# Shared rows scattered into the table of sums, and first-choice blocks scattered onto them with addition

## The chip, the cores and the metric

The kernel runs on one core of a Trainium2 chip, in one launch. Its time is the device time of that core in microseconds (us); smaller is better. The engines are named as in the profile: PE is TensorE (PEld its weight loads), DVE is VectorE, ACT is ScalarE, POOL is GpSimd and SP is SyncE, which here only issues DMAs.

## The reference, cut to what matters

Input x has 8 x 2048 = 16384 tokens of D = 256 float32 values. A time-mixing layer (an RWKV recurrence with four 256 x 256 products) gives a residual, and a mixture-of-experts layer follows. Only the second matters for the change:

```python
probs = softmax(xf @ router_w)            # 8 experts
topw, topi = top_k(probs, 2)              # a first and a second choice per token
h  = silu(einsum('nd,edf->nef', xf, w1))
ye = einsum('nef,efd->ned', h, w2)
routed = einsum('ne,ned->nd', combine, ye)      # weight1 * ye[first] + weight2 * ye[second]
shared = sigmoid(xf @ gate_w) * ((silu(gate) * up) @ shared_down)
x = x + layernorm(routed + shared)
```

So each token ends as a sum of three rows of 256 values: the shared row, the first choice's weighted row and the second choice's weighted row. The norm and the residual come after the sum.

## The kernel before

**First stage (about 0 to 1083 us).** The tokens go through in NCH = 32 chunks of 512. For each chunk the time-mixing layer, the router and the shared expert are computed; every float32 product is made of three matmuls with split operands. For each choice the kernel works out a position for every token in a table that is sorted by expert (`place`, L1151). POOL then scatters rows with indirect DMAs of 128 rows each. `scatter` (L541) writes the normalised token row, with its weights, its second-choice position, its token number and two statistics (272 floats), to `d_xd[0]` at the first-choice position and to `d_xd[1]` at the second-choice position. `shared_scatter` (L553) writes the shared row (256 floats) to `d_xs` at the first-choice position. The gaps between the experts' regions are filled with padding rows by SP (`pads`, L393), whose position fields are out of bounds, so that they are skipped in later scatters.

**Second stage (about 1083 us to the end).** The tables are read in blocks of 256 rows: NB1 = 71 blocks of first choices and then 71 of second choices. `tabx` holds each block's first row and `tabp` its expert. Per block w: SP loads 256 rows of `d_xd` into one of 12 buffers `xb` (`load_block`, L425); PE transposes them (`block_in`), ACT and DVE split them into a high and a low part and copy the expert's weights; PE multiplies (`block_hidden`), ACT applies silu, PE multiplies again (`block_out`) into one of three PSUM buffers `outB`; DVE's `y_out` (L1399) multiplies by the weight and adds a row that SP has loaded into one of 12 buffers `yb` (`load_result`, L435).

For a first-choice block, that loaded row is the shared row from `d_xs`; POOL's `sums_out` (L588) scatters the sum, in two indirect DMAs of 128 rows, into the table of sums `d_ys` at the second-choice positions. For a second-choice block, the loaded row is from `d_ys`; ACT takes squares, POOL computes the scale (`last_scale`), DVE finishes (`final`), and POOL scatters to the output (`tokens_out`).

The order within every engine is the program order. A wait on a semaphore holds back all that stands behind it on that engine. PE may start `block_out(w)` only when `y_out(w - 3)` is done, because there are three `outB`. SP may load into `xb` or `yb` buffer w only when the scatter of block w - 12 has landed (`landed`, L362). The first `load_result` of the second choices (w = NB1 = 71) waits until the scatters of the last 12 first-choice blocks have landed, since the rows that it reads may come from any of them.

Of the kernel before, what the change touches and what calls it, by code (L numbers as in the profile page):

```python
# [5 lines left out]
ALU = mybir.AluOpType  # L6
ACT = mybir.ActivationFunctionType
AX_X = mybir.AxisListType.X
F32 = mybir.dt.float32
# [5 lines left out]
P = 128  # L15
TC = 512
NT = TC // P
# [3 lines left out]
BLK = 256  # L21
XW = 272


def rwkv_moe(nc, x, decay, u_in, mix_k, mix_v, mix_r, wkT, wvT, wrT, woT, router, w1, w2,
# [9 lines left out]
    B, T, D = x.shape  # L35
    E = w1.shape[0]
    H = D // P
    N = B * T
    NCH = N // TC
    assert D == 256 and E == 8 and T == CARRY * TC  # L40
    RW = E + 2
    CAP = N + BLK
# [4 lines left out]
    NB1 = NF + E - 1  # L47
    NB = 2 * NB1
    NBP = NB1 + 1
    NX = NYB = 12  # L50
    LY = 2
    LT = 6
# [4 lines left out]
    x_v = x.rearrange("b (c j p) d -> (b c) p j d", j=NT, p=P)  # L57
    out_r = out.rearrange("b t d -> (b t) d")
    d_xd = [nc.dram_tensor(f"d_xd{s}", [E * CAP + BLK, XW], F32).ap() for s in range(2)]
    d_xs = nc.dram_tensor("d_xs", [E * CAP + BLK, D], F32).ap()  # L60

    d_ys = nc.dram_tensor("d_ys", [E * CAP + BLK, D], F32).ap()

    with ExitStack() as ctx:
# [80 lines left out]
        ixs = sb("ixs", [P, 2, 2 * NT], U32)  # L145
# [85 lines left out]
        s_T1 = sem("s_T1")  # L231
# [32 lines left out]
        s_h2 = sem("s_h2")  # L264
# [18 lines left out]
        s_scy = sem("s_scy")  # L283
# [5 lines left out]
        s_pad = sem("s_pad")  # L289
        s_xb = [sem(f"s_xb{i}") for i in range(NX)]  # L290
        s_yo = [sem(f"s_yo{i}") for i in range(NYB)]
        s_yl = [sem(f"s_yl{i}") for i in range(NYB)]
# [10 lines left out]
        s_y = sem("s_y")  # L303
# [21 lines left out]
        def n(c, per, k):  # L325
            return c * per + k

        def rows(t):
# [5 lines left out]
        xb = [old[i // 5][:, i % 5 * 2 * XW:(i % 5 + 1) * 2 * XW] for i in range(10)] + [t[:, 0:2 * XW] for t in old[2:4]]  # L334
        xb = [t.rearrange("p (j d) -> p j d", j=2) for t in xb]
        sil = [flat(t)[:, i * 2 * D:(i + 1) * 2 * D] for t, i in ((al, 0), (be, 0), (al, 1))]
        hidB, outB = PS[2:5], PS[5:8]
        yb = [flat(t)[:, i * 2 * D:(i + 1) * 2 * D].rearrange("p (j d) -> p j d", j=2)
              for i in range(2) for t in (kk, vv, tr, dl, nx, x1)]
# [22 lines left out]
        def landed(w):  # L362

            return s_yo[w % NYB], 32 * (w // NYB + 1)
# [6 lines left out]
        @block.sync  # L371
        def _(sp):
            def load_weights(m):
                for i, src in enumerate(loads[m]):
                    w = src.shape[2]
                    dst = flat(stage[m])[:, i * H * w:(i + 1) * H * w]
                    sp.dma_start(dst.rearrange("p (a n) -> p a n", a=H), src).then_inc(s_wld[m], 16)

            sp.dma_start(xin[:, :, :], x_v[0]).then_inc(s_x, 16)
            with nc.allow_non_contiguous_dma(reason="small vectors, once"):  # L380
                for i, v in enumerate((mix_k, mix_v, mix_r)):
                    sp.dma_start(vec[:, i, :], v.rearrange("o t (a p) -> p (o t a)", p=P)).then_inc(s_vec, 16)
                load_weights(0)
                for i, v in enumerate((u_in, decay)):
                    sp.dma_start(vec[:, 3 + i, :], v.rearrange("(a p) -> p a", p=P)).then_inc(s_wu, 16)
                load_weights(1)
                sp.wait_ge(s_const, NCONST)
                sp.dma_start(rwf[:, :, 0:E], src_mat(router)).then_inc(s_rwf, 16)
                sp.dma_start(rwf[:, :, E:E + 1], src_mat(gate_w)).then_inc(s_rwf, 16)
                load_weights(2)  # L390
                load_weights(3)

            def pads(e):  # L393

                sp.wait_ge(s_zt, 2)
                for rows, width in ((d_xd[0], XW), (d_xd[1], XW), (d_xs, D), (d_ys, D)):
                    pad = rows[e * CAP:e * CAP + BLK, :].rearrange("(p j) d -> p j d", p=P)
                    sp.dma_start(pad, zt[:, 0:width].unsqueeze(1).to_broadcast([P, 2, width])).then_inc(s_pad, 16)

            sp.wait_ge(s_nx, n(0, NT, NT))  # L400
            sp.dma_start(xin[:, :, :], x_v[1]).then_inc(s_x, 16)
            sp.wait_ge(s_wl, NP)
            sp.dma_start(x1[:, :, :], x_v[0]).then_inc(s_xr, 16)
            for i in range(NCH + 4):
                if i % 2 == 0 and i // 2 < E:

                    raw = wel[:, i // 2 * 1024:(i // 2 + 1) * 1024].bitcast(F32)
                    if i:
                        sp.wait_ge(s_we, 32 * (i // 2))
                    for k, src in enumerate((w1[i // 2], w2[i // 2])):  # L410
                        sp.dma_start(raw[:, k * H * D:(k + 1) * H * D].rearrange("p (a n) -> p a n", a=H), src_mat(src)
                                     ).then_inc(s_we, 16)
                if 1 < i < NCH:
                    sp.wait_ge(s_nx, n(i - 1, NT, NT))
                    sp.dma_start(xin[:, :, :], x_v[i]).then_inc(s_x, 16)
                if 0 < i - 3 < NCH:
                    sp.wait_ge(s_h2, n(i - 3 - 1, NT, NT))
                    sp.dma_start(x1[:, :, :], x_v[i - 3]).then_inc(s_xr, 16)
                if 0 <= i - FIRST_PAD <= E:
                    pads(i - FIRST_PAD)  # L420
            sp.wait_ge(s_pad, 16 * 4 * (E + 1))
            sp.wait_ge(s_tab, 2)
            sp.wait_ge(s_sct[0], 16 * NT * NCH)

            first_row = {}  # L425

            def load_block(b):
                if b >= NX:
                    sp.wait_ge(*landed(b - NX))
                s = b // NB1  # L430
                r = sp.value_load(tabx[0:1, s, b % NB1:b % NB1 + 1], min_val=0, max_val=E * CAP)
                first_row[b % (LT + 1)] = r
                sp.dma_start(xb[b % NX], d_xd[s][bass.ds(r, BLK), :].rearrange("(p j) d -> p j d", p=P)
                             ).then_inc(s_xb[b % NX], 16)

            def load_result(w):

                if w >= NYB:
                    sp.wait_ge(*landed(w - NYB))
                rows_in = d_xs if w < NB1 else d_ys  # L440
                sp.dma_start(yb[w % NYB], rows_in[bass.ds(first_row[w % (LT + 1)], BLK), :].rearrange("(p j) d -> p j d", p=P)
                             ).then_inc(s_yl[w % NYB], 16)

            for b in range(NB + LY):
                if b == NB1:
                    sp.wait_ge(s_tab, 4)
                    sp.wait_ge(s_sct[1], 16 * NT * NCH)
                if b == 10:
                    sp.wait_ge(s_up, n(NCH - 1, 2, 2))
                if b < NB:  # L450
                    load_block(b)
                due = [b - LY] if LY <= b < NB + LY and (b - LY) % NB1 >= LT - LY else []
                if b % NB1 == LT and b < NB:
                    due = list(range(b - LT, b - LY + 1))
                for w in due:
                    if w == 0:
                        sp.wait_ge(s_scy, 16 * NT * NCH)
                    if w == NB1:
                        for k in range(NB1 - NYB, NB1):
                            sp.wait_ge(*landed(k))  # L460
                    load_result(w)

            for w in range(NB - NYB, NB):
                sp.wait_ge(*landed(w))

        @block.gpsimd
        def _(pool):
            g = nc.gpsimd
# [85 lines left out]
            def shared_scatter(m):  # L554
                pool.wait_ge(s_pl, n(m, NPL, L_IX))
                for j in range(NT):
                    pool.wait_ge(s_ys, n(m, NT, j + 1))
                    g.indirect_dma_start(d_xs, bass.IndirectOffsetOnAxis(ap=ixs[:, m % 2, j:j + 1], axis=0),  # L558
                                         ysh_of(m)[:, j, :], None).then_inc(s_scy, 16)

            scale_in(0)
# [25 lines left out]

            def sums_out(w):  # L588

                pool.wait_ge(s_y, 2 * (w + 1))  # L590
                for j in range(2):
                    g.indirect_dma_start(d_ys, rows_at(w, j, C_POS), yb[w % NYB][:, j, :], None,  # L592
                                         bounds_check=E * CAP - 1, oob_is_err=False).then_inc(s_yo[w % NYB], 16)

            def last_scale(q):

# [362 lines left out]
        def _(dve):  # L959
            V = nc.vector  # L960
# [360 lines left out]
            w, y, z = NCH - 3, NCH - 2, NCH - 1  # L1321
# [76 lines left out]

            def y_out(w):  # L1399
                dve.wait_ge(s_yp, w + 1)  # L1400
                dve.wait_ge(s_yl[w % NYB], 16 * (w // NYB + 1))
                col = C_W + w // NB1
                for j in range(2):
                    t = yb[w % NYB][:, j, :]
                    V.scalar_tensor_tensor(out=t, in0=outB[w % 3][:, j * D:(j + 1) * D], scalar=xb[w % NX][:, j, col:col + 1],  # L1405
                                           in1=t, op0=ALU.mult, op1=ALU.add).then_inc(s_y, 1)
# [345 lines left out]
```

## Time and profile before

| what | value |
|---|---|
| median of three runs | 1598.68 us (1597.98 to 1603.28) |
| the profiled execution | 1603.3 us, of which the span is 1601.5 us |
| mean granted PE clock | 0.976 of 2.4 GHz |
| PE busy | 1513.8 us (95%) |
| DVE busy | 1377.2 us (86%) |
| ACT busy | 1336.3 us (83%) |
| POOL busy | 1079.9 us (67%) |
| DMA, software queue (issued by POOL) | 32064 packets, 86.04 MB, 14.6% of 16 engines |
| DMA, hardware queue (issued by SP) | 92368 packets, 126.13 MB, 26.1% of 16 engines |

The span is the time from the first to the last instruction of the profiled execution; the time of the execution is 1.8 us longer. Shares over the whole span mix three stretches with different limits: the chunks (to about 1083 us), the first choices (1083 to 1337 us) and the second choices (from 1337 us), so the text reads the stretches one by one. Busy time of POOL for an indirect DMA is the time in which it writes the DMA's descriptors, not the time in which the data move.

### The profile page before, as it was taken

The page shows a single profiled execution, that of the slowest core. Times are in us where ns is not written, and L with a number is a line of the kernel's source. Part 1 is how long each engine was busy: PE and PEld are TensorE (multiplying, and loading weights), DVE is VectorE, ACT ScalarE, POOL GpSimd, SP SyncE. Part 2 cuts the span into 40 slices and gives each one's busy share as a digit, 9 for nine tenths or more (in the row PEclk, how much of TensorE's full clock was granted, in tenths as well). Part 3 has the DMA queues.
Part 4 walks back from the last instruction along what each step waited for, and adds up shares of the span by engine and source line. Part 5 has one row for each costly group of instructions (what it writes and reads, how often), then busy time and mean ns, then how long its engine had stood idle before and what let it go on. Part 6 is the DMA issues. An engine that isn't in the chain of part 4 may idle for free.

```text
span 1601.5 us, 35130 instructions
## 1 busy us (share of the span) xinstructions
PE 1513.8 (95%) x9960; PEld 1360.9 (85%) x9960; DVE 1377.2 (86%) x3140; ACT 1336.3 (83%) x2768; POOL 1079.9 (67%) x1168
## 2 busy tenths in 40 slices
PE   5899999999999999999999999689999998999992
PEld 4778888888888888888888888578999998999992
DVE  5899998999999999999999888856877777999993
ACT  5688998899889988999898888756777777999993
POOL 1256677767776766677677766766666664888886
PEclk9999999999999999999999999889999999999996
DMA  4114333533322222222222222138777764777771
GB/s 125 41 55 132 118 113 115 171 106 126 108 95 82 83 85 91 79 86 87 88 82 82 91 72 73 65 100 283 238 238 244 247 207 136 229 223 229 235 239 55
DMA packets 124619, 214.41 MB, mean 134 GB/s; under 512 B 19975, under 2 KB 67338, under 8 KB 124432
## 3 DMA queue, kind: packets, MB, share of 16 engines
q1 hardware_dynamic: 92368, 126.13, 26.1%
q0 software_dynamic: 32064, 86.04, 14.6%
q8 instruction: 86, 1.41, 0.4%
q14 instruction: 101, 0.83, 0.2%
HBM read 116.37 MB, written 99.39 MB: 135 GB/s over the span
## 4 chain that ended last, share of the span: by engine, by line
PE 62%; DVE 12%; issue 10%; POOL 9%; ACT 1%; DMA 1%; DVEq 1%; POOLq 0%; SPq 0%; ACTq 0%
PE PS L1474 53%; POOL d_ys L592 8%; PE PS L1466 3%; PE PS L1538 2%; PE PS L1536 2%; PE PS L1692 2%; DVE rkl L1446 1%; DVE shl L1446 1%; PE PS L1708 1%; DVE x L1405 1%; DVE ysh L1413 1%; DVE dl L1405 1%; DVE xin L1413 1%; POOL out L610 1%; DVE tr L1405 1%
## 5 line engine op out<-in xcount | busy, mean ns | idle before, releaser
L551 POOL DMA_INDIRECT d_xd<-h2n,ixs x248 | 310.3, 1251 | 193.2 <-DVE h2n L1193 127.0
L1474 PE MATMUL PS<-hTh,wqh 128*128 128x512 f32 x768 | 305.1, 397 | 12.3 <-DVE hTl L1114 10.3
L1474 PE MATMUL PS<-hTl,wqh 128*128 128x512 f32 x768 | 305.0, 397 | 0.0
L1474 PE MATMUL PS<-hTh,wql 128*128 128x512 f32 x768 | 305.0, 397 | 0.0
L1474 PEld LDWEIGHTS PS<-hTh,wqh 128*128 128x128 f32 x768 | 145.9, 190 | 46.4 <-issue 10.9
L1474 PEld LDWEIGHTS PS<-hTh,wql 128*128 128x128 f32 x768 | 145.4, 189 | 34.2
L1474 PEld LDWEIGHTS PS<-hTl,wqh 128*128 128x128 f32 x768 | 145.7, 190 | 33.2
L558 POOL DMA_INDIRECT d_xs<-ysh,ixs x124 | 130.6, 1054 | 45.8 <-issue 45.8
L1708 PE MATMUL PS<-weh,h2h 128*128 x380 | 106.4, 280 | 0.0
L1708 PE MATMUL PS<-weh,h2l 128*128 x380 | 106.3, 280 | 0.0
L1708 PE MATMUL PS<-wel,h2h 128*128 x380 | 106.1, 279 | 0.0
L1474 PE MATMUL PS<-h2h,wgh 128*128 128x512 f32 x248 | 103.4, 417 | 0.0
L1452 DVE TENSOR_TENSOR h2l<-al,h2h 128x512 fp32r<-128x512 f32 x95 | 65.6, 691 | 43.6 <-ACT h2h L953 43.6
L1474 PE MATMUL PS<-h2l,wgh 128*128 128x512 f32 x248 | 97.8, 394 | 0.0
L1474 PE MATMUL PS<-h2h,wgl 128*128 128x512 f32 x248 | 97.5, 393 | 0.0
L1692 PE MATMUL PS<-rkh 128*128 128x256 f32 x284 | 86.3, 304 | 5.7 <-DVE rkl L1446 5.5
L1474 PE MATMUL PS<-woh,rkh 128*128 128x256 f32 x256 | 76.4, 298 | 15.0 <-DVE rkl L1211 15.0
L1692 PE MATMUL PS<-hTh,shh 128*128 128x256 f32 x284 | 86.3, 304 | 3.5 <-DVE shl L1446 3.5
L1692 PE MATMUL PS<-rkh,rkl 128*128 128x256 f32 x284 | 80.8, 284 | 0.0
L1692 PE MATMUL PS<-rkl,rkh 128*128 128x256 f32 x284 | 80.7, 284 | 0.0
L1692 PE MATMUL PS<-hTl,shh 128*128 128x256 f32 x284 | 80.6, 284 | 0.0
L1041 DVE TENSOR_TENSOR_SCAN ee<-negw,ee,kk 128x512 f32<-128x512 f32 x64 | 78.7, 1272 | 1.9 <-ACT kk L647 0.6
(330 smaller groups left out, 5665.8 us busy)
## 6 DMA issues: line engine op xcount, KB each, us to landing
xin<-in_L_attn_x SPq DMA_DIRECT2D x32, 512.0 KB, 4.3
x<-in_L_attn_x SPq DMA_DIRECT2D x32, 512.0 KB
wqh<-d_xd SPq DMA_DIRECT2D x60, 272.0 KB, 3.5
wql<-d_xd SPq DMA_DIRECT2D x60, 272.0 KB, 2.9
d_xd<-zt SPq DMA_DIRECT2D x18, 272.0 KB
wel<-in_L_ffn_w SPq DMA_DIRECT2D x16, 256.0 KB, 5.1
d_xd<-h2n,ixs POOLq DMA_INDIRECT x248, 2.6
kk<-d_xs SPq DMA_DIRECT2D x12, 256.0 KB
```

What stands on the lines that cost most here:

```text
L551: g.indirect_dma_start(d_xd[s], bass.IndirectOffsetOnAxis(ap=ixs[:, m % 2, k:k + 1], axis=0), h2n_of(m)[:, j, :], None).then_inc(s_sct[s], 16)
L558: g.indirect_dma_start(d_xs, bass.IndirectOffsetOnAxis(ap=ixs[:, m % 2, j:j + 1], axis=0), ysh_of(m)[:, j, :], None).then_inc(s_scy, 16)
L592: g.indirect_dma_start(d_ys, rows_at(w, j, C_POS), yb[w % NYB][:, j, :], None, bounds_check=E * CAP - 1, oob_is_err=False).then_inc(s_yo[w ...
L1041: V.tensor_tensor_scan(ee[:, a, 1:TC + 1], negw[:, a:a + 1].to_broadcast([P, TC]), kk[:, a, :], ee[:, a, 0:1], ALU.add, ALU.max).then_inc( ...
L1405: V.scalar_tensor_tensor(out=t, in0=outB[w % 3][:, j * D:(j + 1) * D], scalar=xb[w % NX][:, j, col:col + 1], in1=t, op0=ALU.mult, op1=ALU. ...
L1413: V.tensor_scalar(xk[v % 4][:, 0, :], xb[w % NX][:, 0, 0:D], xb[w % NX][:, 0, C_EXT:C_EXT + 1], xb[w % NX][:, 0, C_EXT + 1:C_EXT + 2], ALU ...
L1446: V.tensor_copy(w1l[t % 2], wel[:, bass.ds(base, H * D)]).then_inc(s_w1l, 1)
L1452: V.tensor_tensor(aTl[u % 3], sil[u % 3], aTh[u % 3].bitcast(F32), ALU.subtract).then_inc(s_al2, 1)
L1466: ins = nc.tensor.transpose(bank[a][:, j * P:(j + 1) * P], src[:, j, a * P:(a + 1) * P], ident[:, :])
L1474: ins = mm_(out_ap, l, r, start=(k == 0), stop=(k == len(todo) - 1))
L1692: ins = mm_(hidB[u % 3][:, f * D:(f + 1) * D], l, r, start=(k == 0), stop=(k == len(todo) - 1))
L1708: ins = mm_(outB[w % 3][:, j * D:(j + 1) * D], l, r, start=(k == 0), stop=(k == len(todo) - 1))
```

## The change

The table `d_xs` goes. In the first stage, `shared_scatter` writes the shared rows into `d_ys`, at the second-choice positions (columns NT to 2 NT of `ixs`, where it used columns 0 to NT). First-choice blocks no longer load anything into `yb`: `y_out` writes weight x product there by a `tensor_scalar`, and `sums_out` scatters it with `compute_op=ALU.add`, so that the DMA adds the row to what `d_ys` holds. The wait for all the shared scatters moves from SP (ahead of the first `load_result`) to POOL (ahead of the first `sums_out`). The wait that buffer `yb` is free again moves, for first-choice blocks, from SP to DVE. Second-choice blocks are as before, and SP's list of result loads starts with w = 71.

```diff
-    d_xs = nc.dram_tensor("d_xs", [E * CAP + BLK, D], F32).ap()
...
-                for rows, width in ((d_xd[0], XW), (d_xd[1], XW), (d_xs, D), (d_ys, D)):
+                for rows, width in ((d_xd[0], XW), (d_xd[1], XW), (d_ys, D)):
...
-            sp.wait_ge(s_pad, 16 * 4 * (E + 1))
+            sp.wait_ge(s_pad, 16 * 3 * (E + 1))
...
-                rows_in = d_xs if w < NB1 else d_ys
-                sp.dma_start(yb[w % NYB], rows_in[bass.ds(first_row[w % (LT + 1)], BLK), :].rearrange("(p j) d -> p j d", p=P)
+                sp.dma_start(yb[w % NYB], d_ys[bass.ds(first_row[w % (LT + 1)], BLK), :].rearrange("(p j) d -> p j d", p=P)
                              ).then_inc(s_yl[w % NYB], 16)
...
-                due = [b - LY] if LY <= b < NB + LY and (b - LY) % NB1 >= LT - LY else []
-                if b % NB1 == LT and b < NB:
+                due = [b - LY] if b - LY >= NB1 + LT - LY else []
+                if b == NB1 + LT:
                     due = list(range(b - LT, b - LY + 1))
                 for w in due:
-                    if w == 0:
-                        sp.wait_ge(s_scy, 16 * NT * NCH)
...
             def shared_scatter(m):
-                    g.indirect_dma_start(d_xs, bass.IndirectOffsetOnAxis(ap=ixs[:, m % 2, j:j + 1], axis=0),
+                    g.indirect_dma_start(d_ys, bass.IndirectOffsetOnAxis(ap=ixs[:, m % 2, NT + j:NT + j + 1], axis=0),
                                          ysh_of(m)[:, j, :], None).then_inc(s_scy, 16)
...
             def sums_out(w):
+                if w == 0:
+                    pool.wait_ge(s_scy, 16 * NT * NCH)
                 pool.wait_ge(s_y, 2 * (w + 1))
                 for j in range(2):
                     g.indirect_dma_start(d_ys, rows_at(w, j, C_POS), yb[w % NYB][:, j, :], None,
-                                         bounds_check=E * CAP - 1, oob_is_err=False).then_inc(s_yo[w % NYB], 16)
+                                         bounds_check=E * CAP - 1, oob_is_err=False, compute_op=ALU.add).then_inc(s_yo[w % NYB], 16)
...
             def y_out(w):
                 dve.wait_ge(s_yp, w + 1)
-                dve.wait_ge(s_yl[w % NYB], 16 * (w // NYB + 1))
                 col = C_W + w // NB1
+                if w < NB1:
+                    if w == 0:
+                        dve.wait_ge(s_h2, n(NCH - 1, NT, NT))
+                        dve.wait_ge(s_T1, n(NCH - 1, 2, 2))
+                    if w >= NYB:
+                        dve.wait_ge(*landed(w - NYB))
+                    for j in range(2):
+                        V.tensor_scalar(yb[w % NYB][:, j, :], outB[w % 3][:, j * D:(j + 1) * D], xb[w % NX][:, j, col:col + 1],
+                                        None, ALU.mult).then_inc(s_y, 1)
+                    return
+                dve.wait_ge(s_yl[w % NYB], 16 * ((w - NB1) // NYB + 1))
```

## Rows read from the trace of the kernel before

**Rows 1.** Windows by stage: us, busy time (instructions) per engine, granted clock, DMA share, GB/s.
```profile
1080.00:1120.00 40.00, 36.16 (x285) 35.53 (x285) 25.08 (x50) 27.00 (x48) 26.19 (x26) 0.93 0.84 283
1200.00:1320.00 120.00, 120.00 (x1032) 120.00 (x1031) 88.59 (x184) 88.47 (x148) 81.28 (x74) 1.00 0.74 236
1320.00:1360.00 40.00, 35.65 (x283) 34.97 (x282) 29.28 (x66) 31.23 (x75) 17.12 (x19) 0.91 0.40 130
```

**Rows 2.** Waits, 1200 to 1320 us: who waited for whom, total us, times, longest.
```profile
POOL d_ys L592 <- issue: 33.3, 68, 0.7
DVE h2l L1452 <- ACT h2h L953: 20.4, 24, 1.0
ACT hTh L941 <- PE PS L1673: 11.1, 19, 0.6
```

**Rows 3.** Timeline, POOL, in step with the blocks: start, us, instruction [idle before <- releaser].
```profile
1318.27 0.98 POOL L592 DMA_INDIRECT d_ys<-vv,wql  x1 [0.72 <-issue]
1319.56 1.23 POOL L592 DMA_INDIRECT d_ys<-vv,wql  x1 [0.30 <-issue]
1321.52 0.99 POOL L592 DMA_INDIRECT d_ys<-tr,wql  x1 [0.72 <-issue]
```

**Rows 4.** Timeline, POOL, late and without a wait between blocks.
```profile
1285.11 0.99 POOL L592 DMA_INDIRECT d_ys<-tr,wql  x1 [1.81 <-DVE dl L1405]
1286.40 0.99 POOL L592 DMA_INDIRECT d_ys<-dl,wql  x1 [0.30 <-issue]
1287.69 0.99 POOL L592 DMA_INDIRECT d_ys<-dl,wql  x1 [0.30 <-issue]
1288.99 0.99 POOL L592 DMA_INDIRECT d_ys<-nx,wgh  x1 [0.30 <-issue]
```

**Rows 5.** Tile d_xs: duration ns min/median/max, first and last start.
```profile
L558 POOL DMA_INDIRECT d_xs<-ysh,ixs x124: 956/963/1877, 152.5 to 1082.8; - x124
L398 SPq DMA_DIRECT2D d_xs<-zt x9: 643/658/1723, 151.6 to 406.1; - x9
DMA to landing us min/median/max: 3.1/3.8/4.9
```

**Rows 6.** Windows at the end of the first choices, and where only loads run.
```profile
1318.00:1332.00 14.00, 14.00 (x123) 14.00 (x122) 8.42 (x18) 10.63 (x18) 8.95 (x8) 1.00 0.13 41
1335.00:1341.00 6.00, 3.83 (x18) 3.86 (x19) 4.71 (x11) 3.25 (x9) 0.00 (x0) 0.50 0.98 333
```

**Rows 7.** Timeline, from the last scatter of first choices to the second choices.
```profile
1329.34 1.28 POOL L592 DMA_INDIRECT d_ys<-nx,wgh  x1 [0.30 <-issue]
1332.02 0.33 SPq L441 DMA_DIRECT2D x<-d_ys  x1
1334.94 0.88 DVE L1405 SCALAR_TENSOR_TENSOR x<-PS,wgl,x 128x256 f32<-128x256 f32 x2 [5.19 <-DMA x<-d_ys]
1335.73 0.40 DVE L1413 TENSOR_SCALAR ysh<-wgl 128x256 f32<-128x256 f32 x1
1337.17 0.55 PE L1692 MATMUL PS<-rkh 128*128 128x256 f32 x1 [4.35 <-DVE rkl L1446]
1341.79 0.32 PE L1708 MATMUL PS<-weh,shh 128*128 x1
```

**Rows 8.** Timeline, start of the first choices.
```profile
1088.01 0.96 POOL L558 DMA_INDIRECT d_xs<-xin,ixs  x1 [0.30 <-issue]
1090.55 0.33 SPq L441 DMA_DIRECT2D kk<-d_xs  x1
1092.32 0.35 PE L1692 MATMUL PS<-hTh,shh 128*128 128x256 f32 x1 [0.76 <-DVE shl L1446]
1095.91 0.87 DVE L1405 SCALAR_TENSOR_TENSOR kk<-PS,wqh,kk 128x256 f32<-128x256 f32 x2
1097.60 1.00 POOL L592 DMA_INDIRECT d_ys<-kk,wqh  x1 [3.07 <-DVE kk L1405]
1115.77 0.36 PE L1692 MATMUL PS<-rkh 128*128 128x256 f32 x1 [0.35 <-DVE rkl L1446]
1129.82 0.36 PE L1692 MATMUL PS<-rkh 128*128 128x256 f32 x1 [0.45 <-DVE rkl L1446]
```

## The prediction

> **What bounds the kernel now.** The change lies in the first choices, 1083 to 1337 us, and touches the first stage only in where rows go; so I read the busy time by window first, then the waits of that stretch, then POOL's timeline, and last the two seams, where the stretch begins and where it ends.
>
> Between 1200 and 1320 us PE is busy for 120.00 of 120 us at the full clock [rows 1]. POOL issues 74 indirect DMAs there, two per block, so 37 blocks take 120 us: 3.24 us per block. The waits agree that nothing holds PE: none has PE as the waiter, DVE's largest is 20.4 us for ACT, ACT's is for PE [rows 2]. This stretch is bound by PE alone.
>
> POOL needs care. Its timeline looks full: pairs of DMAs, 0.72 us between blocks and 0.30 us inside a pair [rows 3]. The reader may take that for a bound, since the wait view calls all of it "issue" [rows 2]. But when POOL was 1.81 us late it went from one block to the next with 0.30 us, and each DMA took 0.99 us [rows 4]. So a pair costs 2 x (0.99 + 0.30) = 2.58 us when POOL does not wait, against the block's 3.24 us. POOL has 0.66 us to spare per block, 0.33 us per DMA. It follows DVE in step, and its second DMA is stretched to 1.23 us, which costs nothing.
>
> The DMA engines are 74% busy at 236 GB/s [rows 1]. Where only loads run they reach 333 GB/s at 0.98 [rows 6]. They are a resource with a quarter to spare.
>
> **Part by part, first stage.** The shared scatter keeps its count of 128 DMAs of 128 rows; its row has a median of 963 ns and only the index column changes [rows 5]. The nine padding stores of `d_xs` go, 0.66 us of SP's queue each, between 152 and 406 us [rows 5]; SP has no arithmetic and nothing waits on that stretch of its queue but the next x load, which is a chunk ahead. Both: 0.
>
> **Loads removed.** 71 loads of 256 KB go from SP, at 0.33 us of issue each and a landing of 3.1 to 4.9 us [rows 5, 8]. They are issued blocks ahead: in the whole stretch from 1200 to 1320 us no wait names them [rows 2]. At the start, SP's first `d_xs` load went at 1090.55 us, and DVE used it at 1095.91 us, right after PE's product [rows 8]. Nothing is gained there but DMA time. Per block: 256 KB at 333 GB/s is 262,144 / 333,000 = 0.79 us.
>
> **DVE.** Two `scalar_tensor_tensor` of 0.44 us (0.88 us for two) become two `tensor_scalar`; the nearest row, the same width from SBUF, has 0.40 us [rows 7]. I take a gain of 0.08 us per block, bounds 0 and 0.2. DVE has 88.59 of 120 us of work [rows 1], so it is hidden: 0.
>
> **Moved waits.** POOL's new wait for all shared scatters: the last one was issued at 1088.01 us, and SP's load of 1090.55 us stood behind that same semaphore; POOL's first sum goes at 1097.60 us [rows 8]. It passes with 7 us to spare; had the cover gone, the pairs of all 71 blocks would queue behind it. DVE's new wait for the landing of block w - 12: behind it stand the splits of the next block, for which PE waits. It has 12 x 3.24 = 39 us of cover against a landing of a few us. Both 0, as long as POOL and the DMA engines keep pace.
>
> **The addition: POOL.** The trace has no scatter with addition. Lower end: it costs what the same scatter without addition costs, 0.99 us [rows 4]. Upper end: it costs two such DMAs, because each row names two things to read, 1.98 us. A saving is excluded, since it still names every row. PE's pace is lost from 3.24 / 2 - 0.30 = 1.32 us on. I take 1.15 us, nearest to its own row with addition for the second address, and so no cost in the steady stretch; the second of a pair takes 1.23 us today and nobody waits [rows 3].
>
> **The addition: DMA engines.** A block now moves 272 KB of x, 256 KB of shared rows and 256 KB of sums. The busy time is 0.74 x 3.24 = 2.40 us per block [rows 1]; the two loads are 541 KB at 333 GB/s, 1.62 us, so the plain scatter has 0.78 us. Afterwards: x at 0.84 us plus a scatter with addition at k x 0.78 us. Read and write of the same rows is k = 2, which gives 2.40 us again, the same load as today. k = 1 gives 1.62 us. PE's pace is lost from k = (3.24 - 0.84) / 0.78 = 3.1 on; the trace has no row that bounds k from above. I take 2.
>
> **The seam to the second choices.** This is the one place where the scatter is on the path. The last scatter is issued until 1330.62 us, the load of block 71 goes at 1332.02 us, DVE gets it at 1334.94 us, and PE stands still for 4.35 us and then runs at half clock (1.2 GHz) until 1341.79 us [rows 7]. Here the longer POOL span counts twice (two DMAs of the last pair): 2 x (1.15 - 0.99) = 0.3 us. The landing could grow too, but 41 GB/s from 1318 to 1332 us [rows 6] say that the last blocks are nearly all padding and move next to nothing; I add 0.3 us, bounds 0 and 2. Sum: 0 + 0.3 + 0.3 - 0.1 (DVE's shorter step) = +0.5 us.
>
> **Sum.** The profiled execution took 1603.3 us (span 1601.5), 4.6 us above the median of 1598.7; it is the slowest of the three runs. On it: 1603.3 + 0.5 = 1603.8. Carried to the median: 1598.7 + 0.5 = 1599.2, rounded to 1599.5 us. The case's own range is 1595 to 1604.
>
> **Rivals.**
>
> *POOL becomes the bound (slower).* Mechanism: writing descriptors for a row that is read twice takes long enough that a pair exceeds 3.24 us; POOL then sets the pace of all 71 first-choice blocks, the lag piles up in the 12 buffers, and the first load of the second choices has to wait it out, so all of it is paid. It decides from 1.32 us per DMA. At one and a half times today's span, 1.48 us, a pair takes 2 x 1.78 = 3.56 us: 71 x 0.32 = 23 us, 1622 us. At 1.98 us it is 4.56 us: 71 x 1.32 = 94 us, 1693 us. For it: the slack is only a third of a span. Against it: the span hardly varies with the rows (963 ns for the shared rows, 990 ns with a bounds check [rows 4, 5]), which speaks for a large fixed part.
>
> The Trainium skill speaks for this rival: "GPSIMD Engine Reference", section "When to use GPSIMD", has one core write the read descriptors and another the write descriptors, and "Collectives: The Full Stack", section "The bandwidth ceiling", has an add on the DMA path take two read descriptors where a copy takes one. By these the reading side's share would double, and the time would fall anywhere between this rival's ends; no run here shows a DMA with addition yet.
>
> *The DMA engines become the bound (slower).* If read, add and write of a row cost k = 4 plain rows, a block needs 0.84 + 3.12 = 3.96 us: 0.72 us over, and over the some 67 blocks that move data (the last four by the 41 GB/s do not) 48 us, 1647 us. For it: rows of 1 KB are short, and an addition must wait for its own read. Against: at k = 2 a quarter of the engines' time stays free.
>
> *Faster.* What the removed loads crowd would come earlier: PE's gaps at the start, 0.76 + 0.35 + 0.45 us [rows 8], and at the seam 4.35 us and the half clock from 1337.17 to 1341.79 us (2.3 us lost). All gone, that is 8.2 us: 1590.5 us. Against: the gaps at the start are waits for DVE's and ACT's splits, and the seam's wait is for a scatter that stays.
>
> **How the numbers follow.** No change (POOL keeps pace): 0.45. POOL bound: 0.35. DMA bound: 0.14. Faster: 0.06. The likeliest single case gives the time, 1599.5 us, though the two slower ones together weigh a little more. A measurement here tells 0.3%, 4.8 us, from no change. Of the first case 0.42 falls within that, 0.02 above, 0.01 below; of POOL bound 0.03 within (a pair barely above the pace); of the faster case 0.05 beyond and 0.01 within. That is faster 0.06, same 0.46, slower 0.48. The range must take in most of POOL's case and the nearer part of the DMA engines': 1594 to 1665 us leaves out about 0.04 below and 0.14 above.
>
> **What would show it.** POOL's indirect DMA on `d_ys` in the first choices: a span under 1.32 us and idle time of 0.4 us or more between pairs bears me out; 0.30 us everywhere with a longer span is the POOL rival. A block period of 3.24 us between 1200 and 1320 us with PE at 120 of 120 is the core of the forecast. A DMA share near 0.74 shows k = 2; near 1.0 with DVE waiting for landed scatters shows the DMA rival. At the seam, PE's gap should be 4 to 6 us. I am wrong if PE shows gaps inside the first choices.

## The result and the profile after

The changed kernel takes 1637.76 us (median of 4 runs, 1633.45 to 1640.75) against 1598.86 us for the kernel before in the same comparison: ratio 1.0218, 95% interval 1.0191 to 1.0245. It is 2.2% slower, and the interval is far from no change. The profiled executions took 1639.4 us (span 1637.6) and 1603.3 us (span 1601.5), 36.1 us apart; the text below works on these two.

The windows by stage of the changed kernel (us, busy time and instructions of PE, PEld, DVE, ACT, POOL, granted clock, DMA share, GB/s):

```profile
1160.00:1200.00 40.00, 40.00 (x345) 40.00 (x344) 30.12 (x62) 29.29 (x50) 33.60 (x22) 1.00 0.83 141
1200.00:1320.00 120.00, 109.91 (x914) 106.70 (x914) 83.39 (x164) 78.74 (x132) 100.49 (x65) 1.00 0.85 142
1320.00:1360.00 40.00, 28.30 (x234) 27.07 (x232) 18.66 (x36) 19.96 (x33) 33.60 (x22) 0.93 0.75 124
```

The stretch from the first scatter of sums to the stop of PE at the seam, in the changed kernel and then in the kernel before:

```profile
1098.25:1351.95 253.70, 238.63 (x2000) 233.36 (x1998) 181.86 (x364) 172.25 (x286) 213.00 (x134) 1.00 0.83 138
```
```profile
1097.60:1332.82 235.22, 234.26 (x2002) 233.19 (x2000) 175.28 (x364) 172.03 (x286) 157.65 (x142) 1.00 0.72 231
```

PE, full in the middle of the first choices before [rows 1], now has gaps: none from 1160 to 1200 us, 10 of 120 us after that. The window from 1320 us also holds the first 8 us of the wait at the seam. Over the whole stretch PE is idle for 15.1 us, and was for 1.0 us. POOL issued 74 DMAs in 120 us before; now it issues 65, and is busy for 100 us. The reader should see the order: POOL is at its limit from the start, PE only later, because the 12 buffers let POOL fall behind for a while.

POOL's timeline in the same stretch, and its last pair with the load behind it:

```profile
1256.06 1.55 POOL L590 DMA_INDIRECT d_ys<-x,wql  x1 [0.30 <-issue]
1257.92 1.55 POOL L590 DMA_INDIRECT d_ys<-kk,wql  x1 [0.30 <-issue]
1259.78 1.55 POOL L590 DMA_INDIRECT d_ys<-kk,wql  x1 [0.30 <-issue]
...
1365.11 1.55 POOL L590 DMA_INDIRECT d_ys<-nx,wgh  x1 [0.30 <-issue]
1368.12 0.33 SPq L439 DMA_DIRECT2D x<-d_ys  x1
1370.89 0.88 DVE L1413 SCALAR_TENSOR_TENSOR x<-PS,wgl,x 128x256 f32<-128x256 f32 x2 [22.39 <-DMA x<-d_ys]
1373.12 0.55 PE L1700 MATMUL PS<-rkh 128*128 128x256 f32 x1 [21.17 <-DVE rkl L1454]
```

Each DMA with addition takes 1.55 us where the plain one took 0.99 us [rows 4], and there are 0.30 us between any two, also between blocks, where POOL used to stand idle for 0.72 us [rows 3]. The first scatter of the first choices starts at 1098.25 us, the last ends at 1366.66 us: 268.4 us for 71 blocks, 3.78 us each. Before, it was 1097.60 to 1330.62 us [rows 7, 8]: 233.0 us, 3.28 us each. The difference, 35.4 us, is the loss. The start came 0.65 us later. The seam itself is the same: 1.4 us from the last scatter's end to the load, 2.8 us to DVE (2.9 before), 2.2 us to PE, as before [rows 7]; only PE's gap is longer (21.17 us, not 4.35), since it now waits out the lag that POOL had built up. So 16.8 us of the loss are a longer wait at the seam and 14.1 us are PE's gaps before it; PE's busy time in the stretch grew by the other 4.4. From PE's restart to the end of the span there are 264.5 us, and were 264.3 us.

Some of the waits (who waited for whom, us in total, times, longest), POOL's of 1085 to 1390 us, PE's and SP's of the stretch up to the seam, show how the lag reaches PE:

```profile
POOL d_ys L590 <- issue: 37.8, 124, 0.3
```
```profile
PE PS L1681 <- DMA wql<-d_xd: 5.2, 7, 1.5
SPq L430 <- DMA d_ys<-x,wql: 18.9, 6, 3.9
```

After its first scatter POOL waits for nothing that is longer than its own 0.30 us. PE's transposes (L1681) wait for x rows, 13.6 us in all (this line and three like it). SP in turn waits at its own queue for scatters to `d_ys` (L430): each x load stands behind the landing of the scatter 12 blocks earlier, which POOL has not got to.

### The profile page after: what moved, and what is told of

It is laid out like the page before. It is cut to its first block, busy times and chain, and to the rows that moved or that the text cites. A ratio compares the mean times of both kernels' runs of the same rounds, so it can differ in the third digit from the quotient of the medians.

```text
span 1637.6 us, 34898 instructions
## 1 busy us (share of the span) xinstructions
PE 1521.6 (93%) x9960; PEld 1364.0 (83%) x9960; DVE 1383.4 (84%) x3140; ACT 1336.3 (82%) x2768; POOL 1143.9 (70%) x1168
## 3 DMA queue, kind: packets, MB, share of 16 engines
q0 software_dynamic: 45696, 86.05, 20.2%
q8 instruction: 86, 1.41, 0.4%
## 4 chain that ended last, share of the span: by engine, by line
PE 66%; DVE 12%; issue 9%; POOL 5%; DMA 4%; ACT 2%; DVEq 1%; SPq 0%; POOLq 0%; ACTq 0%
PE PS L1482 52%; PE PS L1700 4%; POOL d_ys L590 3%; PE PS L1474 3%; PE PS L1716 2%; PE PS L1546 2%; PE PS L1544 2%; PE PS L1681 1%; DVE rkl L1454 1%; DVE shl L1454 1%; DVE ysh L1421 1%; DVE xin L1421 1%; POOL out L608 1%; DVE tr L1413 1%; DVE x L1413 1%
## 5 line engine op out<-in xcount | busy, mean ns | idle before, releaser
L554 POOL DMA_INDIRECT d_ys<-ysh,ixs x124 | 130.7, 1054 | 45.8 <-issue 45.5
```

Of the source, the lines that this page charges most:

```text
L554: g.indirect_dma_start(d_ys, bass.IndirectOffsetOnAxis(ap=ixs[:, m % 2, NT + j:NT + j + 1], axis=0), ysh_of(m)[:, j, :], None).then_inc(s_ ...
```

## Experiments

The theory after the result: POOL's time to write the descriptors of an addition is the pace of the first choices. Its rival: the DMA engines that read, add and write the rows are the limit (their share rose from 0.74 to 0.85). A second rival: the moved waits cost something of their own.

A measure that all the runs below share is the length of the first choices, from POOL's first scatter of sums to PE's first matmul after the seam: 239.6 us before, 274.9 us changed. In the comparisons below the kernel before had medians of 1602.9 to 1603.6 us, 4 to 5 us above the one that the expectations start from, so the ratios say more than the absolute times.

**e1, the addition left out.**

```diff
-   oob_is_err=False, compute_op=ALU.add)
+   oob_is_err=False)
```

> The changed kernel with a plain scatter instead of one with addition (the shared rows are lost from the sums). POOL theory (writing descriptors for an addition takes 1.55 us per DMA, 3.70 us per pair, against PE's 3.24 us per block): the span falls back to 0.99 us and the time to about 1599 us (1596 to 1603). Rival, the rest of the change costs something (the moved waits on DVE and POOL): more than 1604 us. The DMA theory says 1599 us too.

Measured: 1603.14 us, ratio 1.0005 (0.9979 to 1.0030).

```profile
1200.00:1320.00 120.00, 120.00 (x1032) 120.00 (x1030) 89.01 (x185) 89.13 (x148) 81.36 (x74) 1.00 0.53 160
```

Spans are mostly 0.98 to 0.99 us again for the first of a pair, PE is full, and the first choices take 239.0 us. So the new destination, the missing loads and the moved waits cost nothing, and gain nothing either; the whole loss hangs on `compute_op`.

**e2, the addition kept, its rows skipped.**

```diff
-   bounds_check=E * CAP - 1, oob_is_err=False, compute_op=ALU.add)
+   bounds_check=0, oob_is_err=False, compute_op=ALU.add)
```

> The changed kernel with its addition kept, but with a bound of 0, so that every row of it is skipped and no sums are moved (the routed first choice is lost). POOL theory: POOL still writes 1.55 us per DMA, and the time stays at 1633 to 1639 us. DMA theory (the engines that read, add and write the rows set the pace, and POOL is held by them): without rows to move the time falls to about 1599 us, and POOL's span with it.

Measured: 1639.71 us, 0.7 above the range, ratio 1.0225 (1.0206 to 1.0244), the changed kernel's own loss, with a DMA share of 0.32. Window and a POOL row of this run:

```profile
1200.00:1320.00 120.00, 111.43 (x917) 107.05 (x916) 83.60 (x165) 79.66 (x132) 100.80 (x64) 1.00 0.32 77
...
1249.03 1.55 POOL L590 DMA_INDIRECT d_ys<-nx,wqh  x1 [0.30 <-issue]
```

No sum is moved, and of these numbers only the DMA share changes; the first choices take 275.4 us (274.9 in the changed kernel). So the span of 1.55 us does not come from moving the rows, and it sets the pace without them. This is the run that tells the two theories apart.

**e3, addition in every second scatter.**

```diff
+   how = dict(compute_op=ALU.add) if j else {}
-   bounds_check=E * CAP - 1, oob_is_err=False, compute_op=ALU.add)
+   bounds_check=E * CAP - 1, oob_is_err=False, **how)
```

> The changed kernel with addition in the second scatter of each pair only; the first is plain (half of the shared rows are lost). POOL theory, with the pace of PE as a threshold: a pair takes 0.99 + 0.30 + 1.55 + 0.30 = 3.14 us, below 3.24 us, so nearly the whole loss goes: 1599 to 1604 us. If half of the additions cost half of the loss, with no threshold: about 1618 us.

Measured: 1610.61 us, ratio 1.0042 (1.0028 to 1.0055); above the 1604 us expected, well below 1618. In the first choices the threshold holds:

```profile
1200.00:1320.00 120.00, 120.00 (x1031) 120.00 (x1031) 88.78 (x185) 89.14 (x148) 97.46 (x74) 1.00 0.76 161
...
1253.65 1.03 POOL L591 DMA_INDIRECT d_ys<-kk,wqh  x1 [0.30 <-issue]
1254.99 1.65 POOL L591 DMA_INDIRECT d_ys<-kk,wqh  x1 [0.30 <-issue]
1256.94 1.04 POOL L591 DMA_INDIRECT d_ys<-vv,wqh  x1 [0.30 <-issue]
```

PE is full, POOL issues 74 DMAs, and the first choices take 240.5 us. A pair takes 3.29 us here (1253.65 to 1256.94), just PE's pace. The 7 us above the kernel before lie in the second choices, where this kernel's code is that of the others: 274.2 us from PE's restart, not 264.3 (the first choices began 3.2 us earlier here). Some POOL scatters there take 1.6 to 1.76 us from 1495 us on. Why is open (last section).

**e4, a third plain scatter with nothing to move, in the kernel before.**

```diff
+   g.indirect_dma_start(d_ys, rows_at(w, 0, C_POS), yb[w % NYB][:, 0, :], None,
+                        bounds_check=0, oob_is_err=False).then_inc(s_yo[w % NYB], 16)
...
```

> The kernel before with a third plain scatter per first-choice block whose rows are all skipped: no addition anywhere, no more data moved, only POOL's time. POOL theory: three DMAs take 3 x 1.29 = 3.87 us per block against 3.24 us, 71 x 0.6 = 43 us, about 1642 us (1636 to 1648). Theory that the loss is a matter of the addition or of moving rows: 1599 us.

In this kernel the waits for landed scatters count the third one too.

Measured: ratio 1.0385 (1.0366 to 1.0404), 1665.5 us.

```profile
1200.00:1320.00 120.00, 103.03 (x840) 98.11 (x838) 77.11 (x149) 72.64 (x120) 92.58 (x91) 1.00 0.62 196
```

PE loses 17 of 120 us, at a DMA share below that of the kernel before. The mechanism is confirmed without any addition, the size was too low. In the profiled execution (1659.9 us, the shortest of four) POOL runs from 1097.73 to 1381.13 us, 3.99 us per block and not 3.87 (a span of 1.0 to 1.5 us now and then), which makes 50 us in the first choices, and the second choices take 270.7 us, 6.4 more.

**e5 and e6, one and two more loads of 256 KB per first-choice block, in the kernel before.** The rows go to tiles that are idle there; SP waits for the load four earlier, and ACT and DVE for the last loads before they use the tiles again.

```diff
+   if w < NB1:
+       for k in range(1):        # e6: range(2)
...
+           sp.dma_start(xk[u % 4], rows_in[bass.ds(first_row[w % (LT + 1)], BLK), :].rearrange("(p j) d -> p j d", p=P)
+                        ).then_inc(s_du[u % 4], 16)
```

> The kernel before with one more load of 256 KB per first-choice block (its rows are not used): the DMA engines get 2.40 + 0.79 = 3.19 us of work per block, about what they have with the additions at PE's pace, while POOL keeps its plain scatters. POOL theory: 0 to 0.5% longer, under 1608 us, since 3.19 us still fits into 3.24 us. DMA theory (the engines were already at their limit in the changed kernel): about the changed kernel's loss, 1630 us or more.

> The kernel before with two more loads of 256 KB per first-choice block: 2.40 + 1.58 = 3.98 us of DMA work per block against PE's 3.24 us. A control: if the engines' time is counted rightly, the loss is 0.74 us for some 67 blocks, about 50 us, near 1650 us. If it stays below 1610 us, the DMA share overstates how full the engines are, and the DMA rival was further away than counted.

Measured: e5 1602.58 us, ratio 0.9975 (0.9939 to 1.0011); e6 1608.40 us, ratio 1.0014 (0.9984 to 1.0044). The same window of e5, then of e6:

```profile
1200.00:1320.00 120.00, 120.00 (x1031) 120.00 (x1030) 88.68 (x185) 88.04 (x147) 81.96 (x74) 1.00 0.93 309
```
```profile
1200.00:1320.00 120.00, 119.46 (x1018) 118.64 (x1017) 88.65 (x183) 87.81 (x146) 80.23 (x73) 1.00 1.04 394
```

e5 came out as the POOL theory has it. e6 went by its second branch: no 50 us, and under 1610 us. The engines moved 394 GB/s, where I had taken 333 GB/s for full, and the share went above 1, so it does not say how full they are. For loads of 2 KB and more per partition a DMA share of 0.98 was not the limit. But e6 is not free of loss either: its first choices took 244.8 us, 5.2 more than before, most of it PE's gaps between 1100 and 1120 us (16.34 us busy, 19.65 before), at 383 GB/s.

**e7, 64 rows per scatter, the first plain and the second with addition.**

```diff
-   g.indirect_dma_start(d_ys, rows_at(w, j, C_POS), yb[w % NYB][:, j, :], None, ..., compute_op=ALU.add)
+   at = bass.IndirectOffsetOnAxis(ap=xb[w % NX][0:64, j, C_POS:C_POS + 1].bitcast(U32), axis=0)
+   how = dict(compute_op=ALU.add) if j else {}
+   g.indirect_dma_start(d_ys, at, yb[w % NYB][0:64, j, :], None, ..., **how)
```

> The changed kernel with 64 rows in place of 128 per scatter; the first of each pair is plain, the second adds (half of the rows' sums are lost). It splits POOL's span into a fixed part and a part per row. If the addition costs per row (a descriptor more for each), the plain span falls from 0.99 and the adding one from 1.55 so that the gap of 0.56 us halves to about 0.28 us; if it is a fixed cost per DMA, the gap stays 0.56 us. The time should be 1599 to 1604 us in both cases.

```profile
1097.60 0.93 POOL L592 DMA_INDIRECT d_ys<-kk,wqh  x1 [3.28 <-DVE kk L1409]
1098.84 1.73 POOL L592 DMA_INDIRECT d_ys<-kk,wqh  x1 [0.30 <-issue]
...
1250.88 1.26 POOL L592 DMA_INDIRECT d_ys<-nx,wgh  x1 [0.30 <-issue]
1252.44 1.42 POOL L592 DMA_INDIRECT d_ys<-nx,wgh  x1 [0.30 <-DVE x L1409]
```

The spans come in two lengths of each kind: a plain one mostly takes 0.93 to 0.95 or 1.2 to 1.28 us, an adding one 1.41 to 1.45 or 1.64 to 1.76 us. I compare the shorter ones. With half the rows the plain span falls from 0.99 to 0.93 us and the adding one from 1.55 to 1.41 us. With a straight line through these two sizes, a row costs POOL an estimated 0.9 ns plain and 2.2 ns with addition, and what is fixed is 0.87 us and 1.27 us. The gap of 0.56 us shrinks only to 0.48 us: neither of the two expectations, but near the second. By this line most of the extra time (0.40 of 0.56 us) is paid per DMA, whatever it moves. The single run took 1607.05 us, 3 us above what was expected; its first choices took 241.1 us, with PE at 120.00 of 120 us.

The rows from 1250 us also show 0.30 us between any two DMAs, as in e3, although PE sets the pace. A pair of the shorter spans would take 0.93 + 1.41 + 0.60 = 2.94 us of a block's 3.24; the longer spans use up the rest.

**e8 and e9, the seam.** Not about the change, but about the one gap that both kernels have. In e8 `y_out`, `back` and `final` (and ACT's squares) come one block later throughout; in e9 only `y_out` and `back` of block 71 do.

```diff
 # e9
-   if 0 <= t - 3 < NB:
-       y_out(t - 3)
+   ready = [t - 3] if t - 3 != NB1 else []
+   if t - 3 == NB1 + 1:
+       ready = [NB1, NB1 + 1]
+   for w in ready: ...
```

> The kernel before with DVE's y_out, back and final, and ACT's last_squares and back_second, one block later in their engines' order (all results kept). At the seam to the second choices PE waits for DVE's split of the next block, which stands behind y_out(71) and its load; one block later that split goes first. If the seam is a matter of this order, PE's gap of 4.35 us shrinks to about 1.1 us (one block of 3.24 us more cover) and the 2.3 us lost at half clock go too: about 5 us less, ratio 0.995 to 0.998. If the load from the table of sums is what PE waits for in any order, the gap stays at 4 us or more and the time within 0.1%.

> The kernel before with one step moved: DVE's y_out and back of block 71 stand one block later, behind the next block's split, and no other block is moved (all results kept). The kernel that moved them for every block kept the gap at the seam, 4.89 us, because the last scatter of the first choices came a block later as well, and its 12 buffers ran out in the second choices. Here neither moves. Order theory: PE's gap of 4.35 us at the seam falls to 1.5 us or less and the half clock behind it mostly goes: 3 to 6 us less, ratio 0.996 to 0.998. If the gap only moves behind the next block: within 0.1%.

Measured: e8 1.0177 (1.0150 to 1.0203), e9 0.9990 (0.9961 to 1.0019). e8 was a mistake in reasoning: the last scatter moved back by a block too, so PE's gap stayed (4.89 us), and the second choices took 293.9 us, as PE began to wait for x rows there. I put that down to the 12 buffers, which don't cover one block more of delay; it was not tried apart. e9 cuts PE's gap from 4.35 to 3.04 us, where 1.5 or less was expected, and its interval contains no change. No version here beats the kernel before for certain.

## Why the prediction was wrong in its time and held in its range

**What failed.** The likeliest case, 1599.5 us, rested on one number: "I take 1.15 us, nearest to its own row with addition for the second address". It measured 1.55 us. That number was read from no row; the bounds from rows were 0.99 and 1.98 us with a threshold of 1.32 us between them, and 1.55 us lies on the far side. The case that came true is the first rival, "POOL becomes the bound", by its own mechanism. Its formula with the measured span gives 71 x (2 x 1.85 - 3.24) = 33 us; the trace has 35.4 us, as some spans are longer (1.585 us in the mean). Its own price, 1622 us at 1.48 us, was low for the same reason. The range held because this rival was named with its mechanism and priced into it, not by chance. What was set against it, 963 and 990 ns, came from two DMAs of 128 rows each, so it could not tell a fixed part from a part per row; e7 is the first run that can.

**What held.** The bound before the change (PE, at 3.24 us per block) and POOL's slack of 0.66 us per block: e1 and e3 keep PE full, e4 exceeds the slack without any addition. The threshold form (no loss below PE's pace, all of it above) is e3's first choices, 240.5 us at a pair of 3.29 us. That the lag is paid in full: 35.4 us. But the seam shows only 16.8 us of it (a gap of 21.17 and not 4.35 us); 14.1 us were paid earlier, by x loads behind scatters that had not landed, which the rival did not name. The removed loads, the padding and the moved waits at nothing: e1.

**What was mis-sized beside it.** DVE's `tensor_scalar` gains nothing: 0.476 us from PSUM, the same as the `scalar_tensor_tensor` that it replaces; I took 0.08 us per block, without effect on the sum. The additions' cost on the DMA engines is above my k = 2: at 3.69 us per block (65 DMAs in 120 us) the share of 0.85 less the 0.32 of e2 is 1.96 us per block, against 1.72 - 1.18 = 0.54 us for the plain scatter by the same account (e1: 0.53 of 3.24 us), or 2.30 against 0.88 us if x is counted at 0.84 us; k is 2.6 to 3.6. It did not matter: POOL was slower, and e6 shows that the engines' limit was further away than 333 GB/s. One sign was too weak: "0.30 us everywhere with a longer span is the POOL rival" is also what e3 and e7 show, with PE at 120.00 of 120 us. PE's gaps decide.

Whether the additions alone would have bound at PE's pace can't be seen while POOL is behind it, and stays open.

The Trainium skill's "GPSIMD Engine Reference" (section "When to use GPSIMD": one core for the read descriptors, one for the write descriptors) with "Collectives: The Full Stack" (section "The bandwidth ceiling": an add takes two read descriptors) pointed to the right rival. e7 does not speak against it for the part that grows with rows, an estimated 2.2 against 0.9 ns; but the larger part of the extra time, 0.40 us by the same estimate, does not grow with rows, and that rule would not have given it. Why the fixed part is longer stays open.

## What to carry to other kernels

An engine that keeps step with the bound engine can look full and still have slack, or look free and have little: take its back-to-back rows where it is late (in step its spans can stretch, as in e3 and e7), compute what a block costs it without waits, and compare that with the pace. When a change replaces an operation on such an engine by one that the trace doesn't show, the chance of a loss is the chance that the unknown exceeds the slack; a guess in the middle of wide bounds is not a row, and here the slack of 0.33 us per DMA should have weighed more than the guess. To tell an engine's issue time from the data that it moves, keep the instruction and take away the data (here, an index bound of 0).

## What the runs showed of the hardware that was not expected

- An indirect DMA with addition holds POOL for 1.55 us at 128 rows and 1.41 us at 64, a plain one for 0.99 and 0.93 us (the shorter spans of each kind). With every row out of bounds it still takes 1.55 us (e2) and 0.99 us (e4).
- An addition makes more packets: 45696 in the software queue against 32064 plain, 96 more for each of 142 DMAs, and the same 45696 with every row skipped (e2).
- In step with DVE the second plain scatter of a pair took mostly 1.1 to 1.4 us (1.23 and 1.28 in [rows 3] and [rows 7]), out of step 0.99 us [rows 4]. In e3 both kinds were stretched (1.04 and 1.59 to 1.65 us). What stretches them was not tried.
- The second choices took 264 us in the kernels before and after, e1 and e2, but 274.2 us in e3 and 270.7 us in e4, with the same code there. In e3 POOL's scatters to the output took up to 1.76 us from 1495 us on. The cause is open.
- One core's DMA engines moved 394 GB/s over 120 us (e6).
